# Cross-attention on one core: the query keys made for two batches at a time, in row halves, instead of one batch at a time with combined weights

## The chip, the core and the metric

The kernel runs on one core of a Trainium2 chip. The metric is the device time of one execution in microseconds. The chip's five engines run side by side and meet at semaphores: TensorE (PE, matmuls; PEld are its weight loads), VectorE (DVE), ScalarE (ACT), GpSimd (POOL) and SyncE (SP), whose queue issues nearly all DMAs. Each engine takes its instructions in order, so an instruction that waits holds back all behind it.

## What is computed

A perceiver block on 32 batches of 64 latents and 1601 context tokens of width 128: cross attention with 16 heads of 64, a self attention, and a quantized feed-forward. Only the first bears on the change:

```python
def _L0_xattn_ref(x, latents, mask, ...):       # x: context (32, 1601, 128), latents (32, 64, 128)
    xn, ln = layernorm(x, ...), layernorm(latents, ...)
    q = ln @ Wq                                 # 16 heads of 64
    kv = concatenate((xn, ln), axis=1) @ Wkv
    k, v = split(kv, 2, axis=-1)
    q, k, v = (heads(q) * scale, heads(k), heads(v))
    sim = einsum('bhid,bhjd->bhij', q, k)
    sim = where(mask_full[:, None, None, :], sim, max_neg)
    out = einsum('bhij,bhjd->bhid', softmax(sim), v)
    return layernorm(out @ Wout, ...)
```

## The kernel before

**Which keys.** The mask keeps only keys near the end of each context. A flag computed at the start picks one of two plans; with these inputs all keys before the last 448 are masked, and the plan WINDOW runs: 448 context keys and the 64 latents, in 8 steps per batch. A body is a pair of batches, 16 steps (0 to 7 the even batch's scores, 8 to 15 the odd one's). Bodies 0 and 1 are written out, 2 to 14 are a loop, 15 is written out again.

**Queries against keys.** The score of a latent against a key is taken as (A ln) . key, where A = Wq Wk^T per head is a 128x128 matrix. The setup forms A for 16 heads and two kinds of keys (context and latents), as fp16 high part a_h and low part a_l (lines 953, 752, 1295). Per batch, 4 query jobs multiply it with the 64 latents: for 8 heads each, three matmuls of 64 columns per head (lines 999, 1000, 1001: high x high, high x low, low x high). ScalarE copies the bank as a high part (qkc_h, line 780, for context keys; qkl_h, line 782, for latent keys), VectorE subtracts it from the bank for the low part (lines 1409, 1411).

**Jobs.** Preparation of the next batch is a row of jobs in two PSUM banks, jbank, used in turn: T (4 transposes of the normalised context, line 992, emptied to xtT_h and xtT_l, lines 770 and 1402), the 4 query jobs, 8 MAX jobs (lines 1014 and 1015: a row's scores for its maximum, reduced by VectorE, line 1415) and MT (the maxima transposed, line 1018, copied to mT, line 1422). A table sets at which step each stands: T at 0, queries at 0, 1, 1, 2, MAX from 2 to 5, MT at 6, the same in both halves of a body. TensorE makes a job when the last but one has been emptied (s_jobs_taken), so one bank is emptied while the other is filled.

**The steps.** In each step TensorE issues scores (lines 1045, 1047, 1049; step 0 adds the mask row, line 1053), then jobs of that step, then the values of two steps before (line 1072, fp32), then jobs of half steps, then the "tail" of the pairs before: ST1 (line 1101), ST2 (line 1109), self attention scores SC (line 1126), PT (transposes, line 1137), PV (line 1144) and small ones. ScalarE takes in each step the jobs of the half step before, the exp of the scores (line 794), the jobs of the step, the copies of the values (lines 800, 807) and its tail: the self attention's exp EXP (line 830) and PT_OUT (line 834). EXP waits for a maximum on VectorE (line 1486) and a subtraction on GpSimd (line 690).

**DMAs.** SP loads per batch the latents lnT, the context raw, ltT and lt, the maxima's row into mrow and into row 127 of qkc_h (lines 471 to 474), and moves the denominators through HBM (lines 482 to 496).

## Time and profile before

| | us |
|---|---|
| median of 3 runs | 965.45 |
| lowest, highest | 964.99, 966.32 |
| the profiled execution | 965.88 |
| its span, first to last instruction | 964.1 |

TensorE is busy in 855.6 us of the span (89%), VectorE in 597.5, ScalarE in 447.2, GpSimd in 189.4. In a timeline row the first number is the start in microseconds from the span's start, the second the time from the first start to the last end of the merged instructions. A matmul's record includes the way through the array, so neighbouring records overlap; what a matmul occupies is the distance between starts. An fp32 matmul stands as two records. "128\*64" behind MATMUL is rows x columns of the array.

### The profile page before, as it was taken

What the parts mean: (1) busy time and instruction counts of PE and PEld (TensorE: products, weight loads), DVE (VectorE), ACT (ScalarE), POOL (GpSimd) and SP (SyncE); (2) the same over time, 40 slices, a digit from 0 to 9 for tenths busy, and PEclk for the clock granted to TensorE, in tenths of its full rate; (3) what the DMA queues carried; (4) which work ended last, traced back from release to release, by engine and by line L of the source; (5) the groups of instructions that cost most, each with busy time, mean ns of one, the idle gap of its engine ahead of it and who ended that gap; (6) DMA issues with size and microseconds to landing.
All of it is one profiled execution on the core that took longest, in us unless ns stands there. A gap on an engine that the chain in (4) does not pass through costs nothing.

```text
span 964.1 us, 23144 instructions
## 1 busy us (share of the span) xinstructions
PE 855.6 (89%) x7999; PEld 487.7 (51%) x7999; DVE 597.5 (62%) x1564; ACT 447.2 (46%) x731; POOL 189.4 (20%) x351
## 2 busy tenths in 40 slices
PE   3658999999999999999999999999999999996452
PEld 3434554554655565646465555555554655555212
DVE  6857655566566656565757575767576666533377
ACT  2423545354545454555555454545454645451133
POOL 3110012121212212222222121212121212121200
PEclk9958999999999999999999999999999999998555
DMA  4221111111011101011111111111111011000001
GB/s 144 67 102 47 41 33 29 33 28 29 20 30 28 31 19 40 17 28 30 28 25 29 30 28 31 28 31 28 31 28 30 18 30 28 15 13 16 2 1 44
DMA packets 94246, 31.53 MB, mean 33 GB/s; under 512 B 77728, under 2 KB 92928, under 8 KB 94080
## 3 DMA queue, kind: packets, MB, share of 16 engines
q1 hardware_dynamic: 93584, 31.00, 13.1%
q8 instruction: 20, 0.33, 0.1%
q10 hardware_dynamic: 624, 0.05, 0.1%
q14 instruction: 18, 0.15, 0.1%
HBM read 26.25 MB, written 4.32 MB: 32 GB/s over the span
## 4 chain that ended last, share of the span: by engine, by line
PE 72%; DVE 16%; ACT 4%; issue 3%; DMA 2%; DVEq 2%; POOL 1%; SPq 0%; POOLq 0%
PE bank L1072 19%; PE bank L1045 7%; PE bank L1101 6%; PE bank L1049 5%; PE bank L1047 5%; PE bank L999 3%; PE bank L1109 3%; PE bank L1144 3%; PE bank L1001 3%; PE bank L1015 3%; PE bank L1000 3%; DVE mx L1415 3%; DVE qkl_l L1411 2%; ACT qkl_h L782 2%; PE bank L992 2%
## 5 line engine op out<-in xcount | busy, mean ns | idle before, releaser
L794 ACT ACTIVATE p<-bank,maskbias 128x512 f32<-128x512 f32 x224 | 154.0, 688 | 262.5 <-PE bank L1049 257.9
L1072 PE MATMUL bank<-p,xv 128*128 128x512 f32 (+1 forms) x512 | 238.1, 617 | 0.0
L1415 DVE TENSOR_REDUCE mx<-bank 128x1 f32<-128x512 f32 x256 | 165.5, 684 | 53.9 <-PE bank L1015 53.7
L1411 DVE TENSOR_TENSOR qkl_l<-bank,qkl_h 128x512 f16<-128x512 f32 x64 | 44.3, 692 | 111.8 <-ACT qkl_h L782 103.1
L999 PE MATMUL bank<-lnT,a_h 128*128 128x64 f16 x1024 | 102.3, 195 | 0.5 <-DVE xtT_l L1402 0.2
L1000 PE MATMUL bank<-lnT,a_h 128*128 128x64 f16 x1024 | 102.0, 194 | 0.0
L1001 PE MATMUL bank<-lnT,a_l 128*128 128x64 f16 x1024 | 102.0, 194 | 0.0
L999 PEld LDWEIGHTS bank<-lnT,a_h 128*128 128x128 f16 x1024 | 92.1, 99 | 18.0 <-issue 13.0
L1000 PEld LDWEIGHTS bank<-lnT,a_h 128*128 128x128 f16 x1024 | 91.9, 99 | 4.0
L1001 PEld LDWEIGHTS bank<-lnT,a_l 128*128 128x128 f16 x1024 | 91.9, 99 | 0.0
L1045 PE MATMUL bank<-qkc_h,xtT_h 128*128 128x512 f16 (+1 forms) x256 | 87.3, 392 | 0.0
L1047 PE MATMUL bank<-qkc_l,xtT_h 128*128 128x512 f16 (+1 forms) x256 | 85.5, 382 | 0.0
L1049 PE MATMUL bank<-qkc_h,xtT_l 128*128 128x512 f16 (+1 forms) x256 | 85.4, 381 | 0.0
L1072 PEld LDWEIGHTS bank<-p,xv 128*128 128x128 f32 (+1 forms) x512 | 75.6, 190 | 15.7 <-issue 8.8
L1101 PEld LDWEIGHTS bank<-arena,wvF 128*64 128x64 f32 x1024 | 56.3, 139 | 50.3 <-issue 50.3
L1015 PE MATMUL bank<-xtT_h,qkc_h 128*128 128x448 f16 x256 | 81.5, 358 | 0.0
L1101 PE MATMUL bank<-arena,wvF 128*64 128x128 f32 x1024 | 71.0, 283 | 4.0 <-DVE arena L1482 4.0
L1014 PE MATMUL bank<-ltT,qkl_h 128*128 128x64 f16 x256 | 50.1, 196 | 16.4 <-ACT p L794 7.0
L1402 DVE TENSOR_TENSOR xtT_l<-bank,xtT_h 128x512 f16<-128x512 f32 x32 | 22.1, 692 | 67.0 <-ACT xtT_h L770 60.2
L642 POOL TENSOR_TENSOR ve<-mv,epsrow 128x4 f32<-128x4 f32 x32 | 6.5, 203 | 269.2 <-DVE mv L1385 269.2
L1014 PEld LDWEIGHTS bank<-ltT,qkl_h 128*128 128x128 f16 x256 | 25.0, 98 | 61.0 <-DVE qkl_l L1411 30.8
L1409 DVE SCALAR_TENSOR_TENSOR qkc_l<-bank,ident,qkc_h 128x512 f16<-128x512 f32 x64 | 47.8, 747 | 5.8 <-ACT qkc_h L780 2.6
(236 smaller groups left out, 1432.4 us busy)
## 6 DMA issues: line engine op xcount, KB each, us to landing
arena<-den_dram SPq DMA_DIRECT2D x64, 128.0 KB, 3.2
raw<-in_ctx SPq DMA_DIRECT2D x32, 192.0 KB, 2.3
raw<-in_ctx SPq DMA_DIRECT2D x64, 32.0 KB, 2.2
lt<-lt_dram SPq DMA_DIRECT2D x64, 31.8 KB, 2.0
arena<-in_L_xattn_Wkv SPq DMA_DIRECT2D x1, 1024.0 KB, 9.5
lnT_dram<-x_all SPq DMA_DIRECT2D x1, 1024.0 KB, 4.0
ltT_dram<-xf_all SPq DMA_DIRECT2D x1, 1024.0 KB, 4.0
ltT<-ltT_dram SPq DMA_DIRECT2D x32, 32.0 KB, 1.8
```

The costliest lines, as they stand in the source:

```text
L794: a.activation(p32[0:r, slot, :], sbank[t % SRING][0:r, :], ACT.Exp, bias=bias).then_inc(s_probs_ready, 1)
L999: mm(bk[:, col], a_h[:, cl, hh, :], lnT[:, 0, :], start=True, stop=False)
L1000: mm(bk[:, col], a_h[:, cl, hh, :], lnT[:, 1, :], start=False, stop=False)
L1001: op = mm(bk[:, col], a_l[:, cl, hh, :], lnT[:, 0, :], start=False, stop=True)
L1014: mm(bk[:, rest:rest + M], qkl_h[:, col], ltT[:, par, 0, :], start=True, stop=True)
L1015: op = mm(bk[:, 0:rest], qkc_h[:, par, col], xtT_h[:, par, 512 * part:plan.KEYS], start=True, stop=True)
L1045: op = mm(dst, keys_h, q_h[:, col], start=True, stop=False)
L1047: op = mm(dst, keys_h, q_l[:, col], start=False, stop=False)
L1049: op = mm(dst, keys_l, q_h[:, col], start=False, stop=tile > 0)
L1072: op = mm(bk[:, :], rows_of[at, :], p32[at, slot, :], start=tile < 2, stop=tile in (0, plan.TILES - 1))
L1101: op = mm(abank[q // 2][E * odd:E * odd + E, (c % 4) * P:(c % 4) * P + P], wvF[:, cl, col], z[:, :, col], start=cl == 0, stop=cl == 1)
L1415: v.tensor_reduce(mx[:, hq_tile, part:part + 1], bk[:, 0:width], AX.X, ALU.max).then_inc(s_jobs_taken, 1)
```

## The change

The combined weights A are gone. The queries are made in two stages, for both batches of the next pair at once (128 columns).

- **QP** (2 jobs, one bank each): q = Wq ln, 4 chunks of two heads per job, three matmuls of 128 columns per chunk (wq_h, wq_l against lnT). Emptied to q_h and q_l in fp16.
- **QC** (2 jobs, two banks each): per head, the 64 rows of the key weights wk_h, wk_l against the 64 rows of q_h, q_l of that head. The even head of a chunk lies in partitions 0 to 63, the odd one in 64 to 127; their matmuls alternate, the even heads' into one bank, the odd heads' into the other. 24 matmuls of 128 columns and 64 rows per job. This is the query against context keys.
- **QL** (2 jobs, two banks each): the same with the weights for latent keys, into qkl_h and qkl_l, which now have a slot per batch.

QC's results go to qkn_h and qkn_l, since the slots of qkc_h and qkc_l are still read; move_queries has SP copy them by two DMAs of 256 KB per batch when the slot's last scores are done. Only the first pair's go straight to qkc_h and qkc_l. The columns are now ordered with all even heads first. A job of n banks waits until all jobs but the last 2 - n have been emptied. The new table puts QP at steps 0 and 1 of a body, QC at 1.5 and 6.5, QL at 8.5 and 9.5, T of the even batch at 7.5 (before 8), MAX from 2.5 and 10.5. Ahead of the first body, START has T, both QP, both QC, both QL, then MAX and MT. The last body has none of the query jobs. In the setup the transposes of Wq and the 32 matmuls for A with their copies go; wq_h, wq_l and wk_h, wk_l are formed instead.

```diff
+        self.START = self.numbered(self.of_batch(0, at["START"]) + self.of_queries(at["START"]))
+        self.BODY = self.numbered(self.of_batch(1, at["ODD"]) + self.of_queries(at["NEXT"]) + self.of_batch(0, at["EVEN"]))
+        self.LAST = self.numbered(self.of_batch(1, at["ODD"]))
...
+    def of_queries(self, at):
+
+        return [(kind, None, half, at[kind][half], banks) for kind, banks in (("QP", 1), ("QC", 2), ("QL", 2)) for half in range(2)]
...
-    T=[0], Q=[0, 1, 1, 2], XV={2: (0, 4)}, MAX=[2, 2.5, 3, 3, 4, 4, 5, 5], MT=6,
...
+    NEXT=dict(QP=[0, 1], QC=[1.5, 6.5], QL=[8.5, 9.5]),
...
-            def load_queries(n):
-                sp.dma_start(lnT[:, :, :], lnT_dram[:, :, bass.ds(n * M, M)].rearrange("s d q -> d s q")).then_inc(s_lnT_loaded, 16)
+            def load_queries(plan, pair):
+                sp.wait_ge(s_jobs_made, plan.queries_through(pair - 1, "QP", 1))
+                sp.dma_start(lnT[:, :, :], lnT_dram[:, :, bass.ds(pair * 2 * M, 2 * M)].rearrange("s d q -> d s q")).then_inc(s_lnT_loaded, 16)
+
+            def move_queries(plan, pair, k):
+
+                sp.wait_ge(s_jobs_taken, plan.queries_through(pair, "QC", 1))
+                sp.wait_ge(s_scores_ready, (pair * 2 + k - 1) * plan.STEPS)
+                sp.dma_start(qkc_h[:, k, :], qkn_h[:, k, :]).then_inc(s_qk_moved[k], 16)
...
+                        if since and k == 0:
+                            move_queries(plan, i, 1)
+                        if k == 1 and not last:
+                            move_queries(plan, i + 1, 0)
+                        if k == 0 and not last:
+                            load_queries(plan, i + 1)
...
+                if kind == "early":
+                    act.wait_ge(s_in_wq, 16)
+                    a.activation(wq_h[:, :], wq_sb, ACT.Copy, scale=Q_IN).then_inc(s_wq_hi, 1)
+                if kind == "wk":
                     act.wait_ge(s_setup_made, setup_made(kind, k))
-                    dst = {"wq": wqT, "wk": wkF[k // 2], "wv": wvF[:, k // 2, :].rearrange("p (c d) -> p c d", d=D)}[kind]
...
+                    if job.kind == "QP":
+                        a.activation(q_h[:, 4 * job.index:4 * job.index + 4, :].rearrange("p c t -> p (c t)"), both[0][:, :], ACT.Copy, scale=Q_OUT).then_inc(s_qk_hi, 1)
+                    if job.kind == "QC":
+
+                        if happened(n - 1):
+                            for k in range(2):
+                                act.wait_ge(s_qk_moved[k], n * 32 - 32)
+                        for odd in range(2):
+                            dst = heads_of(qkc_h if i is None else qkn_h, job.index, odd)
+                            a.activation(dst, by_batch(both[odd]), ACT.Identity, bias=ident[:, 127:128]).then_inc(s_qk_hi, 1)
+                    if job.kind == "QL":
+                        for odd in range(2):
+                            a.activation(heads_of(qkl_h, job.index, odd), by_batch(both[odd]), ACT.Copy).then_inc(s_qk_hi, 1)
 
             def probs(plan, i, k, t):
...
-                    hf, cl = divmod(j - plan.JOB_Q, 2)
-                    for h in range(8):
-                        col, hh = slice(h * M, h * M + M), 8 * hf + h
-                        mm(bk[:, col], a_h[:, cl, hh, :], lnT[:, 0, :], start=True, stop=False)
-                        mm(bk[:, col], a_h[:, cl, hh, :], lnT[:, 1, :], start=False, stop=False)
-                        op = mm(bk[:, col], a_l[:, cl, hh, :], lnT[:, 0, :], start=False, stop=True)
...
+                if happened(g + job.banks - 2):
+                    pe.wait_ge(s_jobs_taken, g + job.banks - 2)
...
+                    for c in range(4 * job.index, 4 * job.index + 4):
+                        to, heads = bk[:, (c % 4) * P:(c % 4) * P + P], slice(c * P, c * P + P)
+                        mm(to, wq_h[:, heads], lnT[:, 0, :], start=True, stop=False)
+                        mm(to, wq_h[:, heads], lnT[:, 1, :], start=False, stop=False)
+                        op = mm(to, wq_l[:, heads], lnT[:, 0, :], start=False, stop=True)
+                if job.kind in ("QC", "QL"):
+                    cl = ("QC", "QL").index(job.kind)
+                    pe.wait_ge(s_jobs_taken, plan.through(i, last, "QP", None, job.index))
+                    for c in range(4 * job.index, 4 * job.index + 4):
+                        to = slice((c % 4) * M, (c % 4) * M + M)
+                        for w, q, first, final in ((wk_h, q_h, True, False), (wk_h, q_l, False, False), (wk_l, q_h, False, True)):
+                            for odd in range(2):
+                                rws = slice(E * odd, E * odd + E)
+                                op = mm(by_batch(both[odd])[:, :, to], w[rws, cl, c, :], q[rws, c, :].rearrange("p (k t) -> p k t", k=2), start=first, stop=final)
...
+                        if happened(b - 1):
+                            pe.wait_ge(s_qk_moved[par], (b - par) * 16)
+                    if part == 0 and hq_tile in (0, 2):
+                        pe.wait_ge(s_jobs_taken, plan.queries_through(n if par == 0 else n - 1, "QL", hq_tile // 2))
...
-            for k in range(8):
-                dve.wait_ge(s_setup_made, setup_made("A", k))
-                dve.wait_ge(s_a_hi, k + 1)
-                v.tensor_tensor(heads_of(a_l, k), by_head(setup_bank("A", k)), heads_of(a_h, k), ALU.subtract).then_inc(s_setup_dve, 1)
+            dve.wait_ge(s_wq_hi, 1)
+            v.scalar_tensor_tensor(wq_l[:, :], wq_sb, Q_IN, wq_h[:, :], ALU.mult, ALU.subtract).then_inc(s_wq_lo, 1)
...
+                    if job.kind == "QC":
+                        for odd in range(2):
+                            dve.wait_ge(s_qk_hi, n * QJOBS + QC_HI[job.index] + odd)
+                            hi, lo = (qkc_h, qkc_l) if i is None else (qkn_h, qkn_l)
+                            v.scalar_tensor_tensor(heads_of(lo, job.index, odd), by_batch(both[odd]), ident[:, 127:128], heads_of(hi, job.index, odd), ALU.add, ALU.subtract).then_inc(s_jobs_taken, 1)
```

TensorE in the loop's body, from the even batch's values at step 0 on. Before (p is p32, the exps; xv the context values):

```order
L1072 MATMUL bank<-p,xv 128x512
L1126 MATMUL bank<-arena,qT 64x512 x4
L1045 MATMUL bank<-qkc_h,xtT_h 64x512 x2
...
L999 MATMUL bank<-lnT,a_h 128x64
L1000 MATMUL bank<-lnT,a_h 128x64
L1001 MATMUL bank<-lnT,a_l 128x64
...
L1072 MATMUL bank<-p,xv 128x512
...
L1045 MATMUL bank<-qkc_h,xtT_h 128x512
```

After (arena is q_h or q_l in the rows of L1064):

```order
L1134 MATMUL bank<-p,xv 128x512
L1188 MATMUL bank<-arena,qT 64x512 x4
L1107 MATMUL bank<-qkc_h,xtT_h 64x512 x2
...
L1055 MATMUL bank<-lnT,wq_l 128x128
...
L1134 MATMUL bank<-p,xv 128x512
...
L1064 MATMUL bank<-arena,wk_h 128x2x64 x4
L1064 MATMUL bank<-arena,wk_l 128x2x64 x2
...
L1107 MATMUL bank<-qkc_h,xtT_h 128x512
L1109 MATMUL bank<-qkc_l,xtT_h 128x512
```

Where two query jobs stood ahead of step 1's values and one ahead of step 2's, QP1 (12 matmuls) now stands ahead of step 1's values and QC0 (24, in two banks) right behind them.

ScalarE in the loop's body, from the self attention's exp (L830, then L890) on. Before:

```order
L830 ACTIVATE arena<-arena 128x1024
...
L794 ACTIVATE p<-bank,zrow 128x512
...
L770 ACTIVATE xtT_h<-bank 128x512
...
L780 ACTIVATE qkc_h<-bank,ident 128x512
L800 ACTIVATE arena<-bank 128x512
...
L834 ACTIVATE arena<-bank 128x512
...
L794 ACTIVATE p<-bank,maskbias 128x512
...
L782 ACTIVATE qkl_h<-bank 128x512
```

After (L894 is PT_OUT, L874 moves the first latents' sums):

```order
L890 ACTIVATE arena<-arena 128x1024
...
L829 ACTIVATE xtT_h<-bank 128x512
...
L854 ACTIVATE p<-bank,zrow 128x512
L860 ACTIVATE arena<-bank 128x512
...
L874 ACTIVATE arena<-arena 128x1024
...
L894 ACTIVATE arena<-bank 128x512
...
L842 ACTIVATE qkl_h<-bank 128x2x256 x2
...
L854 ACTIVATE p<-bank,maskbias 128x512
```

T's copy moved ahead of the first scores' exp, still behind the self attention's exp; the two copies of QL0 stand behind PT_OUT and ahead of the next exp.

ScalarE ahead of the first body. Before:

```order
L770 ACTIVATE xtT_h<-bank 128x512
L780 ACTIVATE qkc_h<-bank,ident 128x512
L782 ACTIVATE qkl_h<-bank 128x512
L780 ACTIVATE qkc_h<-bank,ident 128x512
L782 ACTIVATE qkl_h<-bank 128x512
```

After:

```order
L829 ACTIVATE xtT_h<-bank 128x512
L831 ACTIVATE arena<-bank 128x512 x2
L839 ACTIVATE qkc_h<-bank,ident 128x2x256 x4
L842 ACTIVATE qkl_h<-bank 128x2x256 x4
L854 ACTIVATE p<-bank,zrow 128x512
```

Four copies for one batch's queries became ten for two batches', all ahead of the first exp.

## Rows read from the trace of the kernel before

**Rows 1.** Stretches: us, busy us (count) by engine, PEclk granted clock, DMA share, GB/s.
```profile
53.00:72.00 19.00, 12.72 (x125) 7.04 (x125) 11.27 (x27) 3.17 (x5) 2.92 (x8) 0.59 0.12 33
500.00:600.00 100.00, 97.92 (x948) 55.24 (x945) 64.33 (x164) 49.76 (x84) 22.19 (x40) 1.00 0.12 28
```
**Rows 2.** The mask row's instructions by its line.
```profile
L1053 PE MATMUL bank<-mrow,onesrow x64: 398/398/631, 71.5 to 847.7; 1*64 1x512 f16 x64
```
**Rows 3.** Timeline, TensorE: mask rows of two bodies, two query jobs, values.
```profile
519.29 0.40 PE L1053 MATMUL bank<-mrow,onesrow 1*64 1x512 f16 x2
...
523.64 0.20 PE L999 MATMUL bank<-lnT,a_h 128*128 128x64 f16 x1
...
525.05 1.10 PE L1072 MATMUL bank<-p,xv 128*128 128x512 f32 x2
525.99 0.38 PE L1045 MATMUL bank<-qkc_h,xtT_h 128*128 128x512 f16 x1
...
569.84 0.40 PE L1053 MATMUL bank<-mrow,onesrow 1*64 1x512 f16 x2
```
**Rows 4.** Timeline, TensorE: two neighbouring 512-column matmuls in fp16.
```profile
564.54 0.38 PE L1047 MATMUL bank<-qkc_l,xtT_h 128*128 128x512 f16 x1
564.76 0.38 PE L1049 MATMUL bank<-qkc_h,xtT_l 128*128 128x512 f16 x1
```
**Rows 5.** Timeline, TensorE: values in two row halves, and in one full tile.
```profile
531.03 0.70 PE L1072 MATMUL bank<-p,xv 64*128 64x512 f32 x2
...
531.56 0.59 PE L1072 MATMUL bank<-p,xv 64*128 64x512 f32 x2
...
532.09 1.09 PE L1101 MATMUL bank<-arena,wvF 128*64 128x128 f32 x16
...
561.08 1.02 PE L1072 MATMUL bank<-p,xv 128*128 128x512 f32 x2
561.94 0.27 PE L1148 MATMUL bank<-ident,cx 128*128 128x128 f32 x1
```
**Rows 6.** Timeline, TensorE: values of step 7, then column-halved scores.
```profile
542.67 1.02 PE L1072 MATMUL bank<-p,xv 128*128 128x512 f32 x2
543.62 0.41 PE L1045 MATMUL bank<-qkl_h,ltT 128*64 128x512 f16 x2
```
**Rows 7.** Timeline, ScalarE and VectorE: query jobs emptied.
```profile
524.55 0.60 ACT L782 ACTIVATE qkl_h<-bank 128x512 f16<-128x512 f32 x1
525.25 0.69 ACT L780 ACTIVATE qkc_h<-bank,ident 128x512 f16<-128x512 f32 x1
...
525.97 0.75 DVE L1409 SCALAR_TENSOR_TENSOR qkc_l<-bank,ident,qkc_h 128x512 f16<-128x512 f32 x1
```
**Rows 8.** Timeline, ScalarE: the self attention's exp and PT_OUT.
```profile
545.37 1.06 ACT L830 ACTIVATE arena<-arena 128x1024 f32<-128x1024 f32 x1 [1.81 <-POOL arena L690]
...
549.37 0.61 ACT L834 ACTIVATE arena<-bank 128x512 f32<-128x512 f32 x1
```
**Rows 9.** Timeline, TensorE: a wait at a MAX job; ST2, transposes, scores.
```profile
530.71 0.20 PE L1014 MATMUL bank<-ltT,qkl_h 128*128 128x64 f16 x1 [0.54 <-ACT p L794]
...
546.85 1.95 PE L1109 MATMUL bank<-wout_sb,arena 128*128 128x128 f32 x16
548.64 0.60 PE L1137 MATMUL bank<-ident,arena 128*128 128x128 f32 x4
549.17 0.41 PE L1045 MATMUL bank<-qkc_h,xtT_h 128*64 128x512 f16 x2
```
**Rows 10.** DMA issues: count, KB each, median us from issue to landing.
```profile
raw<-in_ctx SPq DMA_DIRECT2D x32, 192.0 KB, 2.3
```
**Rows 11.** Timeline, VectorE, ahead of the first body: T and the last query job.
```profile
55.16 0.69 DVE L1402 TENSOR_TENSOR xtT_l<-bank,xtT_h 128x512 f16<-128x512 f32 x1 [2.16 <-ACT xtT_h L770]
...
60.46 0.69 DVE L1411 TENSOR_TENSOR qkl_l<-bank,qkl_h 128x512 f16<-128x512 f32 x1 [0.19 <-ACT qkl_h L782]
```
**Rows 12.** VectorE's subtractions for A in the setup, by their line.
```profile
L1295 DVE TENSOR_TENSOR a_l<-bank,a_h x8: 679/682/692, 26.0 to 30.5; 128x512 f16<-128x512 f32 x8
```

More of the change, by code:

```diff
@@ L48 @@
 LATE = dict(scales=4, round=[5, 6], awT=8, fwT=[9, 10], fwdT=11, wdrow=12)
+Q_IN, Q_OUT, K_IN = 2.0 ** 4, 2.0 ** -8, 2.0
+QJOBS = 10
+QP_HI, QC_HI, QL_HI = (1, 2), (3, 5), (7, 9)
+Job = namedtuple("Job", "kind k index at first banks")
 class Plan:
@@ new lines, in prep @@
+            def prep(plan, i, last, t):
+                n = 0 if i is None else i + 1
+                for job in plan.jobs(i, last):
+                    if job.at != t or job.kind in ("MAX", "MT"):
+                        continue
+                    made = plan.base(i) + job.first + job.banks
+                    both = [jbank[(plan.IN_START * (i is not None) + job.first + c) % 2] for c in range(job.banks)]
+                    act.wait_ge(s_jobs_made, made)
+                    if job.kind == "T":
+                        m, width = job.index, min(4, plan.CH - 4 * job.index) * P
+                        a.activation(xtT_h[:, job.k, 512 * m:512 * m + width], both[0][:, 0:width], ACT.Copy).then_inc(s_xtT_hi, 1)
+                    if job.kind == "QP":
[10 more added lines that the diff above has]
+                            a.activation(heads_of(qkl_h, job.index, odd), by_batch(both[odd]), ACT.Copy).then_inc(s_qk_hi, 1)
@@ L1161, in body @@
                         b = i * 2 + k
[L1162 removed]
                         scores(plan, i, k, t)
[L1164 to L1165 removed]
+                        prep(plan, i, last, s)
                         background(plan, i, since, s, before_self_scores)
```

293 lines of the change are left out of this document (142 added, 151 removed).

## The prediction

> **What bounds the kernel now.** I read the stretches first, then TensorE in order of time, then the other engines around each place where the change puts something. In a stretch of the steady loop TensorE is busy 97.9 us of 100 at the granted clock 1.00 (2.4 GHz), VectorE 64 and ScalarE 50 [rows 1]. So whatever TensorE issues, or waits for, is time; VectorE and ScalarE only matter where TensorE catches up with them. The mask row of a batch's first scores (L1053) starts 64 times between 71.5 and 847.7 us, two per batch [rows 2]: 15.5 pairs in 776 us, 50.1 us per pair, with the first two pairs shorter; a body of the loop takes 50.55.
>
> A query job is 24 matmuls of 64 columns. Two of them run from 523.64 to 525.05 us [rows 3]: 1.41 us, 0.70 per job, 29.4 ns per matmul, each with its own weight load. A 512-column matmul takes 0.22 [rows 4]. The line through both gives 0.056 us for 128 columns.
>
> **TensorE's work, per pair.** Removed: 8 jobs x 0.70 = 5.6 us. Added: QP, 2 jobs of 12 matmuls of 128 columns, 24 x 0.056 = 1.34 us. QC and QL, 4 jobs of 24 matmuls, neighbours in different row halves and different banks. Do such halves run together? In the values of a 64-row tile both halves' first parts start together at 531.03, the second parts at 531.56 and the next instruction at 532.09 [rows 5]: 1.06 us for two matmuls of 512 fp32 columns, while one full one takes 0.86 (561.08 to 561.94). They overlap, at 0.53 per part where a full one needs 0.43, a factor of 1.24. For fp16 with 128 columns the trace has no row, so the bounds are 0.056 (full overlap) and 0.070 us (the factor 1.24) for a couple; I take 0.060, since a couple's output and moving rows are narrower than there. 4 x 12 x 0.060 = 2.9 us (2.7 to 3.4). Each entry to or exit from such a shape costs something: after values ending at 542.67 + 0.86 = 543.53 the column-halved scores start at 543.62 [rows 6], while at 561.94 the unhalved successor starts without a gap. 0.09 us, seven new ones (QC0, QL0 and QL1 stand between full shapes, QC1 before a halved one): 0.6 us. TensorE's net: 5.6 - 1.34 - 2.9 - 0.6 = 0.75 us less per pair (0.2 to 1.0).
>
> The Trainium skill (TensorE: Matmul & The Clock Gate, Back-to-back issue gap) gives about 81 ns per 128-column matmul in a stream where each has its weight load. By that QP would cost 1.9 and the couples 3.9 us, 6.4 with the changes of shape, and the net would be 0.8 us more instead of 0.75 less. Rows 3 speak against it: 29.4 ns with a load each.
>
> **New waits, per pair.** A job of two banks waits until every earlier job has been emptied by ScalarE and VectorE. Before, a job waited only for the last but one.
> - QC0 (step 1.5) stands behind QP1 (step 1) with one values matmul between, 0.94 us (525.05 to 525.99) [rows 3]. Emptying one job after TensorE has issued it at 525.05: ScalarE starts at 525.25, VectorE is done at 525.97 + 0.75 = 526.72 [rows 7], 1.67 us; QP1's copies are of the 0.60 and 0.72 kind, 1.55. The wait is 1.55 + 0.04 - 0.94 = **0.65 us**. Behind it on TensorE stand the scores of step 2 and all else.
> - QC1 (6.5) stands behind MT, whose row is copied while the values of step 6 run: nothing.
> - QL0 (8.5) needs T of the even batch (now 7.5) emptied. On ScalarE T's copy stands behind the exp of the self attention (L830), which starts at 545.37 for 1.06 [rows 8], timed by VectorE's maximum and GpSimd's subtraction. I count from the body's mask row at 519.29: the exp ends at 27.1, T's copy at 27.7, VectorE's at 28.4. TensorE: the values of step 7 ended at 543.53, 24.2 after the mask row [rows 6]; the four jobs up to there cost as much as the four before (2 x 0.67 + 2 x 0.72 against 2.8), QC0's wait and three changes of shape bring 0.9, so T starts at 25.1 at the latest; T 0.5, first scores 1.1, values 0.94 and a change: 27.7. Wait 0.7; if the exp keeps its place and TensorE is 0.3 earlier, 1.0. I take **0.85**.
> - QL1 (9.5) needs QL0 emptied, and on ScalarE QL0's two copies stand behind PT_OUT (L834), which waits for the transposes behind ST2. From the transposes (548.64), which end at 549.17 [rows 9]: PT_OUT 549.37 to 549.98 [rows 8], two copies 1.2, VectorE's second 0.69: 551.9. TensorE has scores 0.77 and values 0.94 meanwhile: 550.9. **1.0 us**.
> - The first maxima of a half wait as before: in the old body TensorE loses 0.54 us at 530.71 ahead of a maximum [rows 9], and the same queue of maxima stays; I count -0.1.
>
> Sum 2.4 us (1.2 to 3.2). Pair: 2.4 - 0.75 = +1.65 us; bodies 2 to 14, 13 x 1.65 = **+21.5 us**.
>
> **Copies to the slots.** Two DMAs of 256 KB per batch on SP's queue, ahead of the loads of queries, context and of the denominator rows. A 192 KB load lands 2.3 us after issue [rows 10]; with two issues of 0.6 and 2.6 each is in 4 us after the last scores of the slot's batch, and the first maximum needs it 2.5 steps on, 8 to 10 us. Context loads go out some 3 us later and have four steps to spare. I cost them at nothing; if that cover went, each half would wait the whole excess.
>
> **Start.** The queries of two batches are made before the first maximum, and nothing covers their emptying. Before: T is emptied at 55.16 + 0.69 = 55.85, the last query job at 60.46 + 0.69 = 61.15 [rows 11]: 5.3 us. After: QP0 hides behind T; QP1 1.3 (the stretch's clock is 0.59 [rows 1]) + 0.2 + 0.6 + 0.8 = 2.9; each two-bank job 0.75 to 1.4 + 0.2 + 0.69 + 0.05 + 0.67 + 0.75 + 0.05 = 3.2 to 3.8, four in a row since each waits for the last. 15.5 to 18.1 against 5.3: +10.2 to +12.8, **+11**. The first batch's maxima, shift row and all scores come after it. In the setup VectorE's 8 subtractions of 0.68 (0.60 apart) [rows 12] give way to 4 and one over 1024 columns, some 1.2: -1.2 us. Bodies 0 and 1 wait on latencies, not on TensorE: longer chains against fewer jobs, +0.5 (-2 to +2). The last body has no query jobs: -2.8 of TensorE, less what its other waits keep, **-2**.
>
> Sum: 21.5 + 11 - 1.2 + 0.5 - 2 = +29.8. The profiled execution took 965.88 us (span 964.1), 0.4 above the median of the three runs; 965.9 + 29.8 = 995.7, so **996**.
>
> **Rivals.**
> (a) The row halves do not overlap in fp16: 24 x 0.056 = 1.34 instead of 0.72 per job, +2.5 per pair, of which 0.6 disappears in the wait at QL0; 13 x 1.9 = +25, 1021 us. For it: no fp16 row. Against it: rows 5. 9%.
> (b) A 128-column matmul with new weights costs more than its columns. The nearest dearer row is ST2, 16 fp32 parts of 128 columns between 546.85 and 548.64 [rows 9], 0.112 each; half way from 0.056 to that, 0.084, adds 24 x 0.028 for QP and 48 x 0.024 for the couples, 1.8 per pair, of which 0.6 is again taken out of a wait: 996 + 13 x 1.2 = 1012. Against it: the 64-column jobs show no such charge. 6%. The Trainium skill's figure in the section named above lies near that middle.
> (c) Faster: the three waits vanish, because TensorE's cover at QC0, QL0 and QL1 is longer than the emptying. The place to look is QL0 and QL1, where one late wait can use up the next one's. 13 x -0.75 - 1.2 - 2 + 10 = -3: 962 us. It decides from waits under 0.1 us per pair, since the start and the ends cost 8 us, 0.64 per pair. Against it: 0.94 against 1.59 us at QC0, both from rows. 6%.
> (d) The slots' DMAs come late, for 128 rows of 2 KB land slower than a load or SP sits in another wait: 1 us at each half is +28, 1024 us. For it: SP is one queue. Against it: 8 us of cover. 4%.
> (e) The waits are half of what I count, since one replaces the next: 996 - 15 = 981. 15%; the forecast itself (985 to 1010) 57%. No change to be measured, between (c) and (e): 3%.
>
> **Numbers.** Faster by over 0.2% (about what a measurement of this kernel can tell from no change): 0.07, (c) and its neighbourhood; same 0.03; slower 0.90. Range 978 to 1015: forecast, (e), (b) and the bounds of the couple's price (13 x 0.5) and of the start; (a), (c) and (d) are left out.
>
> **What the profile after will show.** Steady body 52.2 us between two mask rows; TensorE's share in a steady stretch down to some 94% with the clock still 1.00; idle before QC0 0.65, QL0 0.85, QL1 1.0, for VectorE's last copy; 24 QC matmuls in 0.72 us; the mask row of batch 0 at 81 to 82 us instead of 71.5; no wait on the slots' DMAs. Wrong if the couples take 0.11, if the three waits are not there, or if the clock falls in the loop.

## The result, and the profile after

The changed kernel takes 1021.39 us, median of 4 runs (1019.63 to 1022.33), against 965.88 for the kernel before on the same chip: a ratio of 1.057, interval 1.055 to 1.059. It is slower, as forecast, but by 55.5 us where 30 were forecast, and outside the range. The profiled execution took 1020.62 us, its span is 1018.9.

Mask rows cut both spans into the same stretches. Their starts come from the timeline of TensorE (the line is L1115 now). Here are those of the changed kernel at the start of body 0, in its middle, at its end, and at the start of body 2 and of the last body:

```profile
82.40 0.63 PE L1115 MATMUL bank<-mrow,onesrow 1*64 1x512 f16 x2 [1.48 <-DMA qkc_h<-mT]
116.28 0.40 PE L1115 MATMUL bank<-mrow,onesrow 1*64 1x512 f16 x2
136.90 0.40 PE L1115 MATMUL bank<-mrow,onesrow 1*64 1x512 f16 x2 [0.29 <-DMA qkc_h<-mT]
186.78 0.40 PE L1115 MATMUL bank<-mrow,onesrow 1*64 1x512 f16 x2
882.14 0.40 PE L1115 MATMUL bank<-mrow,onesrow 1*64 1x512 f16 x2
904.42 0.40 PE L1115 MATMUL bank<-mrow,onesrow 1*64 1x512 f16 x2
```

And those of the kernel before that [rows 2, 3] lack, the end of body 0 and the start of body 2:

```profile
117.72 0.40 PE L1053 MATMUL bank<-mrow,onesrow 1*64 1x512 f16 x2
165.46 0.40 PE L1053 MATMUL bank<-mrow,onesrow 1*64 1x512 f16 x2
```

With the mask rows of before at 71.53, 822.57 and 847.74 the account is, in us:

| stretch | before | after | difference | forecast |
|---|---|---|---|---|
| up to the first mask row | 71.53 | 82.40 | +10.9 | +9.8 |
| body 0 | 46.19 | 54.50 | +8.3 | both +0.5 |
| body 1 | 47.74 | 49.88 | +2.1 | |
| bodies 2 to 14 | 13 x 50.55 | 13 x 53.49 | +38.3 | +21.5 |
| half of the last body | 25.17 | 22.28 | -2.9 | -2, with the row below |
| the rest | 116.4 | 114.5 | -1.9 | |

So the start is right within 1.1 us, the loop is short by 1.29 us per body, and body 0 by some 8. The timeline of TensorE in one steady body shows where (start, length, then in brackets the idle time ahead and what ended it):

```profile
507.74 0.40 PE L1115 MATMUL bank<-mrow,onesrow 1*64 1x512 f16 x2
508.07 0.66 PE L1046 MATMUL bank<-ident,raw 128*128 128x128 f32 x4
509.82 0.23 PE L1053 MATMUL bank<-lnT,wq_h 128*128 128x128 f16 x1 [1.09 <-DMA lnT<-lnT_dram]
...
513.98 1.08 PE L1134 MATMUL bank<-p,xv 128*128 128x512 f32 x2
515.63 0.29 PE L1064 MATMUL bank<-arena,wk_h 64*128 64x128 f16 x4 [0.57 <-DVE arena L1474]
...
516.40 0.39 PE L1107 MATMUL bank<-qkc_h,xtT_h 128*128 128x512 f16 x1
...
520.04 0.20 PE L1080 MATMUL bank<-ltT,qkl_h 128*128 128x64 f16 x1 [0.32 <-DVE mx L1487]
...
535.59 1.12 PE L1134 MATMUL bank<-p,xv 128*128 128x512 f32 x2
537.43 0.28 PE L1064 MATMUL bank<-arena,wk_h 64*128 64x128 f16 x4 [0.71 <-DVE xtT_l L1470]
...
541.39 1.12 PE L1134 MATMUL bank<-p,xv 128*128 128x512 f32 x2
543.19 0.29 PE L1064 MATMUL bank<-arena,wk_h 64*128 64x128 f16 x4 [0.68 <-DVE qkl_l L1483]
...
545.20 1.13 PE L1134 MATMUL bank<-p,lt 64*128 64x512 f32 x4
546.80 0.19 PE L1080 MATMUL bank<-ltT,qkl_h 128*128 128x64 f16 x1 [0.48 <-DVE qkl_l L1483]
```

A pair of fp32 values matmuls occupies 0.94 us, so QC0 waits 515.63 - 513.98 - 0.94 = 0.71 us, QL0 0.90 and QL1 0.86. These are the three waits of the forecast (0.65, 0.85, 1.0). A QC job is done in 516.40 - 515.63 = 0.77 us with its changes of shape. The wait that the forecast has not is the first: from T to QP0 are 1.75 us, where T's four transposes occupy 0.5, and what ended it is the load of the queries, lnT.

SP's queue in the same place, and the place of the same load in the kernel before:

```profile
506.22 0.54 SPq L514 DMA_DIRECT2D qkc_h<-arena  x1
...
507.69 0.39 SPq L508 DMA_DIRECT2D lnT<-lnT_dram  x1
```
```profile
530.90 0.44 SPq L461 DMA_DIRECT2D lnT<-lnT_dram  x1
```

The load is issued at 507.69, behind the two slot copies, and lands some 2 us later (median 2.0 us for 15 such loads); TensorE wants it at 508.6. From the first copy's issue to the load's are 1.47 us: that time on SP is what puts the load off; its own way is hardly longer than the median of 1.9 us that it takes where it goes ahead of the copies. The kernel before issued it at 530.90 for queries that it made after the mask row at 544.39, 13 us ahead. By groups of waits (us in total, times, longest) it stands 13 times with 1.0 us each (the idle time counts from the end of the record ahead, so it is some 0.15 us shorter than the wait by starts):

```profile
PE bank L1053 <- DMA lnT<-lnT_dram: 13.1, 13, 1.2
```

In body 0 the same load stands behind nine late weight loads as well. SP's first and last issues of that row, then TensorE:

```profile
81.43 0.37 SPq L592 DMA_DIRECT2D arena<-in_L_attn_Wq  x1
...
85.23 0.43 SPq L596 DMA_DIRECT2D arena<-in_L_ffn_w_down  x1
85.70 0.43 SPq L508 DMA_DIRECT2D lnT<-lnT_dram  x1
```
```profile
82.96 1.11 PE L1046 MATMUL bank<-ident,raw 128*128 128x128 f32 x4
88.22 0.26 PE L1053 MATMUL bank<-lnT,wq_h 128*128 128x128 f16 x1 [4.15 <-issue]
...
107.46 0.27 PE L1084 MATMUL bank<-ident,negm 128*8 128x128 f32 x1 [2.48 <-DVE negm L1490]
...
109.70 0.39 PE L1064 MATMUL bank<-arena,wk_h 64*128 64x128 f16 x4 [0.93 <-DVE mT L1494]
```

QP0 waits 4.15 us ("issue" here, but it starts 2.5 us after the load's issue). Later MT waits 2.48 us, which it did before too (2.58), and now QC1, with two banks, waits for MT's copy. The windows of the changed kernel (us, busy us by engine, granted clock, DMA share, GB/s) show the clock at the lower level (0.50, that is 1.2 GHz) from 82 to 90 us, where TensorE waits for the load, and TensorE busy 92.0 of 100 us in the steady loop, where it was 97.9 [rows 1], at the clock 1.00:

```profile
82.00:90.00 8.00, 3.45 (x20) 2.23 (x22) 0.69 (x1) 1.59 (x3) 0.00 (x0) 0.50 0.52 141
104.00:112.00 8.00, 4.59 (x34) 2.08 (x33) 7.52 (x30) 1.48 (x3) 1.25 (x3) 0.77 0.01 2
500.00:600.00 100.00, 92.01 (x765) 48.35 (x763) 60.73 (x155) 48.67 (x84) 21.45 (x38) 1.00 0.18 48
```

### The profile page after: what moved, and what is told of

The parts are those of the page before. It is cut to its first block, busy times and chain, and to the rows that moved or that the text cites. A ratio compares the mean times of both kernels' runs of the same rounds, so it can differ in the third digit from the quotient of the medians.

```text
span 1018.9 us, 20883 instructions
## 1 busy us (share of the span) xinstructions
PE 850.8 (84%) x6775; PEld 456.3 (45%) x6775; DVE 613.7 (60%) x1593; ACT 447.9 (44%) x754; POOL 190.4 (19%) x351
## 4 chain that ended last, share of the span: by engine, by line
PE 58%; DVE 17%; issue 10%; ACT 6%; DMA 4%; POOL 2%; SPq 2%; DVEq 1%; ACTq 0%; POOLq 0%
PE bank L1134 13%; PE bank L1163 6%; PE bank L1064 5%; PE bank L1107 5%; DVE mx L1487 4%; PE bank L1111 3%; PE bank L1109 3%; PE bank L1081 3%; PE bank L1206 3%; PE bank L1171 3%; DMA lnT<-lnT_dram 3%; DVE qkl_l L1483 2%; PE bank L1199 2%; ACT qkl_h L842 2%; PE bank L1188 2%
## 5 line engine op out<-in xcount | busy, mean ns | idle before, releaser
L1483 DVE TENSOR_TENSOR qkl_l<-bank,qkl_h 128x512 f16<-128x512 f32 x64 | 41.2, 686 | 99.6 <-ACT qkl_h L842 99.5
L1081 PE MATMUL bank<-xtT_h,qkc_h 128*128 128x448 f16 x256 | 88.1, 359 | 0.0
L1064 PE MATMUL bank<-arena,wk_h 64*128 64x128 f16 x1024 | 53.3, 224 | 37.5 <-DVE qkl_l L1483 11.7
L1064 PEld LDWEIGHTS bank<-arena,wk_h 64*128 64x128 f16 x1024 | 38.6, 97 | 86.4 <-DVE qkl_l L1483 23.5
L1080 PE MATMUL bank<-ltT,qkl_h 128*128 128x64 f16 x256 | 50.4, 197 | 21.5 <-DVE mx L1487 11.4
L1474 DVE SCALAR_TENSOR_TENSOR arena<-bank,arena 128x512 f16<-128x512 f32 x32 | 22.1, 691 | 59.3 <-ACT arena L831 59.3
L1479 DVE SCALAR_TENSOR_TENSOR arena<-bank,ident,arena 128x512 f16<-128x512 f32 x60 | 42.0, 739 | 20.3 <-ACT arena L839 20.3
L839 ACT ACTIVATE arena<-bank,ident 128x512 f16<-128x512 f32 x60 | 37.9, 683 | 35.6 <-PE bank L1064 35.6
L1064 PE MATMUL bank<-arena,wk_l 64*128 64x128 f16 x512 | 48.9, 223 | 0.0
L860 ACT ACTIVATE arena<-bank 128x512 f32<-128x512 f32 x64 | 38.5, 602 | 13.7 <-PE bank L1134 13.7
```

What stands on the lines that cost most here:

```text
L1064: op = mm(by_batch(both[odd])[:, :, to], w[rws, cl, c, :], q[rws, c, :].rearrange("p (k t) -> p k t", k=2), start=first, stop=final)
L1080: mm(bk[:, rest:rest + M], qkl_h[:, par, col], ltT[:, par, 0, :], start=True, stop=True)
L1081: op = mm(bk[:, 0:rest], qkc_h[:, par, col], xtT_h[:, par, 512 * part:plan.KEYS], start=True, stop=True)
L1479: v.scalar_tensor_tensor(heads_of(lo, job.index, odd), by_batch(both[odd]), ident[:, 127:128], heads_of(hi, job.index, odd), ALU.add, ALU. ...
L1483: v.tensor_tensor(heads_of(qkl_l, job.index, odd), by_batch(both[odd]), heads_of(qkl_h, job.index, odd), ALU.subtract).then_inc(s_jobs_tak ...
```

## Experiments

Times are medians; "before" beside the groups was 966.65, 966.57, 966.28 and 966.79 us. The mask-row periods stand beside them, since they show a loop body free of the start and the end.

| kernel | us | loop body, mean of 13 | body 0 |
|---|---|---|---|
| before | 965.9 | 50.55 | 46.2 |
| changed | 1021.4 | 53.49 | 54.5 |
| load first | 1000.1 | 52.33 | 50.6 |
| + small copies | 999.8 | 52.33 | 50.6 |
| + rows by threes | 1001.4 | 52.36 | 50.4 |
| + rows by twelves | 1025.5 | 53.71 | 51.8 |
| load first, steps | 982.9 | 50.97 | 50.0 |
| load first, T at 7 | 976.8 | 50.45 | 49.8 |
| the same steps, load late | 990.0 | 51.22 | 55.1 |
| T at 7, start turned | 974.7 | 50.45 | 51.4 |
| + maxima apart | 972.8 | 50.54 | 51.1 |
| start turned, maxima late | 966.6 | 49.91 | 51.9 |
| + rounding late | 961.1 | 49.91 | 45.0 |
| before, rounding late | 965.8 | 50.55 | 46.5 |

### The load's place in the queue

```diff
                 load_rows(plan, None, False, 0)
+                load_queries(plan, 1)
...
                         more = not (last and k == 1)
+                        if since and k == 0 and not last:
+                            load_queries(plan, i + 1)
                         if since and k == 0:
                             move_queries(plan, i, 1)
                         if k == 1 and not last:
                             move_queries(plan, i + 1, 0)
-                        if k == 0 and not last:
-                            load_queries(plan, i + 1)
```

> The changed kernel with one order on SP turned: the load of the next pair's queries (lnT) is issued ahead of the two slot copies in every body from the second on, and ahead of the nine late weight loads in the start. Nothing else moves. Theory A, the load's place in SP's queue is the term that the prediction missed: in the loop TensorE waits at the first QP job 1.26 us for this load, in the first body 4.15 us behind the weight loads. Gone: 13 x 1.26 = 16 in the loop, some 1 in body 1, 4 to 6 in body 0 (its tail runs at the lower clock): 1021.4 - 22 = 999 us (996 to 1003), loop body 52.2 us. Rival B, the next wait takes it over (the exp of the self attention and the two-bank jobs keep their own times): the body stays above 52.9 and the time above 1011.

Measured: 1000.08 us (999.22 to 1000.25), 21 us less; the loop body is 52.33 where 52.2 was expected. SP and TensorE at one body's start:

```profile
492.03 0.39 SPq L508 DMA_DIRECT2D lnT<-lnT_dram  x1
492.62 0.55 SPq L514 DMA_DIRECT2D qkc_h<-arena  x1
```
```profile
494.10 0.66 PE L1047 MATMUL bank<-ident,raw 128*128 128x128 f32 x4
494.59 0.22 PE L1054 MATMUL bank<-lnT,wq_h 128*128 128x128 f16 x1
...
495.26 1.09 PE L1135 MATMUL bank<-p,xv 128*128 128x512 f32 x2
```

QP0 follows T at 0.49 us. The load is issued 2.56 us before it is wanted (492.03 to 494.59), and the waits behind did not take the gain over: 1.16 of 1.26 us come back per body. Theory A holds, rival B falls. Counted from the issue of the maxima's row into qkc_h (490.78 here, 504.76 in the changed kernel), the load goes out after 1.25 us instead of 2.93.

### What the slot copies themselves cost

```diff
-                sp.dma_start(qkc_h[:, k, :], qkn_h[:, k, :])
-                sp.dma_start(qkc_l[:, k, :], qkn_l[:, k, :])
+                sp.dma_start(qkc_h[120:128, k, :], qkn_h[120:128, k, :])
+                sp.dma_start(qkc_l[120:128, k, :], qkn_l[120:128, k, :])
```

> As e1_load_first, and each slot copy carries 8 of its 128 rows (120 to 127) instead of all, so 16 KB instead of 256 KB; the other rows of the slots keep the first pair's queries, so the kernel leaves out nearly all of the copying. Issues, waits and their order stay. Theory A: the copies' bytes are hidden, as in the prediction: within 2 us of e1_load_first. Rival C: the copies' traffic costs time (a maximum that waits for the slot, or other transfers that land later beside them): 5 us or more below e1_load_first; at 1 us per half it would be 28.

Measured: 999.77 us (999.62 to 1000.7), body 52.33. A sixteenth of the bytes changes nothing. The copies' transfers are hidden; what cost time in the changed kernel was their place ahead of another transfer. Both copies are still issued here (0.68 and 0.64 us on SP), so this run says nothing on the time of the issues. Their rows in the changed kernel (count, KB each, median us to landing) lie near the 2.3 us of [rows 10]:

```profile
qkc_h<-arena SPq DMA_DIRECT2D x30, 256.0 KB, 2.4
qkc_l<-arena SPq DMA_DIRECT2D x30, 256.0 KB, 2.5
```

### Do the row halves overlap?

```diff
                     for c in range(4 * job.index, 4 * job.index + 4):
                         to = slice((c % 4) * M, (c % 4) * M + M)
-                        for w, q, first, final in ((wk_h, q_h, True, False), (wk_h, q_l, False, False), (wk_l, q_h, False, True)):
-                            for odd in range(2):
+                        for odd in range(2):
+                            for w, q, first, final in ((wk_h, q_h, True, False), (wk_h, q_l, False, False), (wk_l, q_h, False, True)):
```

> As e1_load_first, but in QC and QL jobs the 12 matmuls of the even heads (upper row half) come first and then the 12 of the odd heads (lower row half), so that only one neighbour pair per job is in different halves. Same work, same banks. If the halves overlap in the changed kernel: a job takes 24 x 0.056 = 1.34 us instead of 0.75, +0.6 per job, 4 jobs per pair, of which at QL0 0.6 can disappear in QL1's wait: +1.8 to +2.4 per pair, 14 pairs and four jobs of the start: 25 to 36 us above e1_load_first. Rival, they never overlapped and a couple is cheap for another reason: within 3 us of e1_load_first.

Measured: 1001.42 us (1000.82 to 1003.4), body 52.36 against 52.33: the loop is the same, and QC0 takes 0.79 us to the next instruction (500.61 to 501.40). The edit did not do what its expectation says: the loop over the halves went inside the loop over the four column blocks, so that they alternate by three matmuls. The next kernel puts it outside both.

```diff
-                    for c in range(4 * job.index, 4 * job.index + 4):
+                    for odd in range(2):
+                        for c in range(4 * job.index, 4 * job.index + 4):
...
-                            for odd in range(2):
```

> As e1_load_first, but in each QC and QL job the 12 matmuls of the even heads (upper row half, first bank) come first and then the 12 of the odd heads (lower row half, second bank). e3_rows_apart had in truth grouped them by three and three, since its loop over the heads stood outside, and its records still run in pairs that start 10 ns apart; so it did not take the overlap away. If the overlap is real and reaches over three matmuls but not twelve: 24 x 0.056 = 1.34 us per job instead of 0.73, +0.6 on each of 4 jobs per pair, of which some can disappear in QL1's wait: +1.8 to +2.4 per pair, 25 to 38 us above e1_load_first (1000.1). Rival, a 64-row matmul of 128 columns takes 0.03 us whatever runs beside it: within 3 us of e1_load_first.

Measured: 1025.51 us (1024.91 to 1025.74), 25.4 above the kernel with the load first. The forecast's 0.06 us per couple does rest on an overlap. QC0 in that kernel:

```profile
515.22 0.28 PE L1065 MATMUL bank<-arena,wk_h 64*128 64x128 f16 x2 [0.57 <-DVE arena L1475]
...
515.68 0.32 PE L1065 MATMUL bank<-arena,wk_h 64*128 64x128 f16 x4
515.81 0.25 PE L1065 MATMUL bank<-arena,wk_l 64*128 64x128 f16 x2
...
516.31 0.22 PE L1065 MATMUL bank<-arena,wk_l 64*128 64x128 f16 x1
```

The twelve of the upper half, 0.056 apart, would end theirs at 515.22 + 12 x 0.056 = 515.89. At 515.68 four start together, so the lower half begins four matmuls early; the job's starts span 1.1 us where alternating they span 0.63. In the program two matmuls with wk_h are always followed by one with wk_l; the four with wk_h and two with wk_l in a row are two such groups, one of each half, interleaved. So matmuls of the lower half start ahead of some of the upper half that stand before them in the program, the first of them ahead of three. Groups of three overlap in full, groups of twelve only at their border. The body grows by 1.38 us: four jobs at about 0.46, less what disappears in QL0's wait, 0.71 to 0.25:

```profile
537.49 0.28 PE L1065 MATMUL bank<-arena,wk_h 64*128 64x128 f16 x2 [0.25 <-DVE xtT_l L1471]
```

### The waits of the two-bank jobs

```diff
-    NEXT=dict(QP=[0, 1], QC=[1.5, 6.5], QL=[8.5, 9.5]),
+    NEXT=dict(QP=[0, 0.5], QC=[1.5, 6.5], QL=[9, 10]),
```

> As e1_load_first, with three steps of the table moved: QP1 from 1 to 0.5, QL0 from 8.5 to 9, QL1 from 9.5 to 10. More of TensorE's own work lies between a job and the two-bank job that waits until it is emptied: 1.7 us instead of 0.94 ahead of QC0 (needs 1.6), 1.7 ahead of QL0. Theory A (waits of two-bank jobs are counted right, 0.65 + 0.85 + 1.0, and are a matter of cover): QC0's goes, QL0's goes, QL1's falls to 0.4 to 0.8, the first maximum behind it gains 0.3: 1.2 to 1.9 us per pair, 17 to 26 us below e1_load_first. Rival: they are set by ScalarE's other work (the exp, PT_OUT), whose times don't move: only QC0's goes, 8 us below e1_load_first, or nothing.

Measured: 982.89 us (982.15 to 984.08), 17.2 less. QC0, QL0 and QL1 wait for nothing, and the first maximum behind QL1 waits 0.82 us instead of 0.48. That is Theory A; but five of the loop's bodies, every second one of the later ones, are 1.5 us longer than their neighbours (51.9 and 50.4). The same 4 us in two bodies, 51.9 us apart:

```profile
571.00:575.00 4.00, 3.84 (x41) 2.63 (x41) 2.09 (x6) 0.94 (x3) 0.74 (x2) 0.80 0.11 24
...
623.00:627.00 4.00, 3.93 (x45) 2.70 (x45) 2.81 (x8) 1.16 (x2) 0.74 (x2) 1.00 0.11 24
```
```profile
571.16 0.19 PE L1081 MATMUL bank<-ltT,qkl_h 128*128 128x64 f16 x1 [0.82 <-DVE qkl_l L1484]
...
573.49 0.63 PE L1110 MATMUL bank<-qkc_l,xtT_h 128*128 128x512 f16 x1
573.92 0.63 PE L1112 MATMUL bank<-qkc_h,xtT_l 128*128 128x512 f16 x1
```

Two neighbouring 512-column matmuls stand 0.43 apart instead of 0.22 [rows 4]: the granted clock is at its lower level for some 3.3 us, 2 us behind the wait. In the other body the wait is 0.79 and the clock stays.

QP1, now half a step behind T, waits 0.21 us for T's copy, which it did not before.

The next kernel moves the waits once more, T of the even batch included:

```diff
-    NEXT=dict(QP=[0, 0.5], QC=[1.5, 6.5], QL=[9, 10]),
-    EVEN=dict(T=[7.5], MAX=[10.5, 11, 11, 11.5, 12, 12, 12.5, 13], MT=14)
+    NEXT=dict(QP=[0, 0.5], QC=[1.5, 6.5], QL=[8, 9]),
+    EVEN=dict(T=[7], MAX=[10.5, 11, 11, 11.5, 12, 12, 12.5, 13], MT=14)
```

> As e4_steps, with T of the even batch at step 7 instead of 7.5, QL0 at 8 instead of 9, QL1 at 9 instead of 10. ScalarE's copy of T then stands ahead of the exp of the self attention, QL0's ahead of PT_OUT, and the first maximum (10.5) has 1.5 steps behind QL1 instead of half a step. In e4_steps two things were left in the loop: 0.8 us ahead of the first maximum in every body, and in every second body a stretch of some 3 us at half the granted clock right behind it, 1.5 us. If that stretch comes of the waits just before it, both go: 14 x 0.8 + 7 x 1.5 = 21 us below e4_steps, 962; QL1 may keep 0.3 per pair: 961 to 968. Rival, the clock's fall has nothing to do with that wait: 0.8 per pair only, 971.

Measured: 976.75 us (973.74 to 977.87), far from the 961 to 968 expected. The maximum's wait is gone and so are the falls of the clock in the profiled execution, the fastest of the four (bodies of 50.2 to 50.5), but half a step earlier T runs into QC1:

```profile
606.70 0.65 PE L1047 MATMUL bank<-ident,raw 128*128 128x128 f32 x4 [0.54 <-DVE arena L1480]
```

Without its falls of the clock the kernel with the first table had 50.4 as well: one wait was traded for another, and what was gained is the clock. That it was this wait that made the clock fall is not shown; a later kernel has one as long and no fall.

> The table of e6_steps_t7 in the changed kernel, with its own order on SP (the load of the queries behind the slot copies and behind the weight loads). If the late load and the waits of the two-bank jobs are separate terms, the load's wait stays whole at the first QP job, 1.2 us per body and 4 in the first, and adds to what the steps leave: 20 to 22 us above e6_steps_t7. Rival, the cover that the steps give hides part of it: 12 or less above.

This is the changed kernel with that table alone, and SP as it was. Measured: 990.04 us (989.35 to 991.48), 13.3 above, where 20 to 22 was expected for separate terms and 12 or less for the rival. Between the two. (The profiled executions lie 15.8 apart, since that of the other kernel is its fastest.) Body 0 pays in full (55.1 against 49.8), but in the loop the load costs 0.77 us, not 1.2. QP0 still waits for it,

```profile
494.13 0.23 PE L1053 MATMUL bank<-lnT,wq_h 128*128 128x128 f16 x1 [0.93 <-DMA lnT<-lnT_dram]
```

but QP1's wait of 0.21 for T's copy in the other kernel is gone here: the delay covers it. T's 0.54 and the maxima's 0.29 and 0.31 stay.

### The start, and a version without the loss

```diff
-    START=dict(T=[0], QP=[0, 0], QC=[1, 1], QL=[2, 2], MAX=[3, 3, 3, 3, 4, 4, 4, 5], MT=6),
+    START=dict(T=[0.5], QP=[0, 0], QC=[1, 1], QL=[2, 2], MAX=[3, 3, 3, 3, 4, 4, 4, 5], MT=6),
```

> As e6_steps_t7, and in the start both QP jobs stand ahead of T. TensorE is idle there for 8.5 us, since T waits for the normalised context of batch 0, and the QP jobs need only the latents. They then run in that idle time, and QC0 waits for T alone: the chain of two-bank jobs begins 2.6 us earlier, 2.6 us below e6_steps_t7 (1.5 to 4). Rival, VectorE holds the two copies of QP back behind the context's normalising, which it does first: under 1 us.

Measured: 974.68 us (971.69 to 975.94), 2.1 less, a difference smaller than the 4 us over which the runs of either kernel spread. The mask rows say more. The first comes 2.7 us earlier (79.4 for 82.1), as expected, but 1.6 of it are lost again in body 0, where the even batch's T and the scores behind it now run at the lower clock; the last comes 1.15 earlier (855.55 for 856.70). So 1.1 us are the edit's, below the 1.5 to 4 forecast, and the rest of the 2.1 lies behind the last mask row, where nothing was changed.

Then two tables for the maxima, both with the start turned:

```diff
-    ODD=dict(T=[0], MAX=[2.5, 3, 3, 3.5, 4, 4, 4.5, 5], MT=6),
+    ODD=dict(T=[0], MAX=[2.5, 3, 3.5, 3.5, 4, 4.5, 4.5, 5], MT=6),
...
+    NEXT=dict(QP=[0, 0.5], QC=[1.5, 6.5], QL=[9, 10]),
+    EVEN=dict(T=[7.5], MAX=[11, 11.5, 11.5, 12, 12.5, 12.5, 13, 13], MT=14)
```

> From e7_start, whose loop body of 50.47 us still holds five waits of TensorE: T for QC1's emptying 0.54, a third maximum of each half 0.31 and 0.33, QP1 0.21, the first maximum 0.18. Here T is back at 7.5, QL0 and QL1 are at 9 and 10 as in e4_steps, the first maximum of the even batch goes from 10.5 to 11, so that a whole step lies behind QL1, and in both halves no maximum is issued straight behind the one before the last. Theory (each wait is cover that is missing between a job and the one that needs its bank): T's 0.54 goes, of the first maximum's 0.8 in e4_steps 0.1 to 0.2 stays, the third maxima's 0.6 falls to 0.1 to 0.4: body 49.6 to 49.9, 8 to 11 us below e7_start (974.7): 964 to 967, the time of the kernel before. Rival: the maxima are now so close to the end of the half that MT and the mask row wait, or the clock falls as in e4_steps: 972 or more.

> From e7_start only the maxima's steps are changed (2.5, 3, 3.5, 3.5, 4, 4.5, 4.5, 5 and the same 8 steps later), T stays at 7 and QL at 8 and 9. Takes away the third maxima's 0.31 and 0.33 per body, puts 0 to 0.2 elsewhere: 6 to 9 us below e7_start, 966 to 969. Rival: VectorE is what the maxima wait for, and the wait turns up at a later one: 973 or more.

Measured: 966.55 us (963.83 to 968.37, 12 runs) for the first, as expected (964 to 967) and no difference from before (0.9999, 0.999 to 1.0008); 972.77 (972.5 to 973.12) for the second, next to its rival's 973: the wait at the third maximum turned up as 0.82 at a later one. The first has that too:

```profile
571.42 0.20 PE L1081 MATMUL bank<-ltT,qkl_h 128*128 128x64 f16 x1 [0.82 <-DVE mx L1488]
```

but T, QC and QL wait for nothing, nor does anything wait for the slots, and its steady window is nearly that of [rows 1]:

```profile
500.00:600.00 100.00, 97.15 (x832) 52.74 (x828) 66.39 (x170) 52.11 (x88) 22.22 (x40) 1.00 0.18 49
```

Body 0 is still 51.9 us long. VectorE rounds the late weights there, between the maxima and the copies of MT and QC1.

```diff
-LATE = dict(scales=4, round=[5, 6], awT=8, fwT=[9, 10], fwdT=11, wdrow=12)
+LATE = dict(scales=7, round=[8, 9], awT=8, fwT=[11, 12], fwdT=13, wdrow=14)
```

> As e9_maxima_late, and VectorE's rounding of the late weights in body 0 stands at steps 8 and 9 instead of 5 and 6 (its scales at 7, what follows it two steps later). In e7_start the rounding runs from 99.1 to 105.6 us, between the last maxima and the copies of the first batch's MT and of QC1: MT waits 2.49, QC1 1.11, T 2.24 us, and TensorE's clock falls to 0.50 behind it. Theory: body 0 of the changed kernel is longer than before's (49.8 against 46.2 in e6_steps_t7) because two-bank jobs stand behind that block; out of the way it gives 4 to 7 us below e9_maxima_late: 958 to 962, faster than the kernel before. Rival: what comes at steps 8 and 9 (QL0, the context's moments) waits for it instead: within 2 us of e9_maxima_late.

> The kernel before, with the rounding of the late weights at steps 8 and 9 of body 0 (scales 7, the rest two steps later), the same edit as in e11_round_late. There too MT waits 2.58 us in body 0 behind that block, but no two-bank job stands behind it, and body 0 lasts 46.19 us. Theory: the block cost the changed kernel more (6.9 us of body 0, by the mask rows of e9_maxima_late and e11_round_late) because QC1 and T wait for whole banks behind it and the clock falls; before gains only MT's wait, 2 to 3 us: 963 to 965. Rival: the rounding costs both the same: 959 to 961, and e11_round_late is no faster than this kernel.

Measured: 961.09 us (959.39 to 962.79), where 958 to 962 was expected, a ratio of 0.995 (0.993 to 0.996): the fastest kernel of the study. The kernel before with the same edit takes 965.79 (963.22 to 967.66), a ratio of 0.999 (0.998 to 1.000), 1 us where 2 to 3 was expected. So to move the block is worth 5.5 us here and about 1 in the kernel before. There the first half of body 0 became 3 us shorter (22.06 for 25.13), as MT's wait fell from 2.58 to 0.41, and the second gave 3.4 back (24.46 for 21.06): its first maximum now waits 2.38 us for the last query job's copy instead of 0.21. In the other kernel the first half of body 0 fell from 29.2 to 22.4 us, and the second stayed at 22.7; it has a new wait of 1.50 at its first maximum too, but its granted clock rose from 0.92 to 1.00. Why the two differ in that was not tested. The middle of body 0, without and with the edit:

```profile
109.65 0.63 PE L1116 MATMUL bank<-mrow,onesrow 1*64 1x512 f16 x2
```
```profile
102.59 0.40 PE L1116 MATMUL bank<-mrow,onesrow 1*64 1x512 f16 x2
```

Body 0 began at 80.5 and at 80.2.

## Why the prediction was off

- **The step that failed** is the sentence on the copies to the slots: "Two DMAs of 256 KB per batch on SP's queue, ahead of the loads of queries, context and of the denominator rows ... I cost them at nothing". The copies themselves were rightly costed at nothing (small copies: 0.3 us less in 1000), and the cover of the maximum and of the context loads was checked. For the load of the queries, which the same sentence names, no time of need was worked out. Before, it had 13 us; now TensorE wants it 0.9 us after its issue. It cost 1.16 us in each loop body, and with body 0's weight loads ahead of it 3.9 there and 2.9 in body 1 (54.5 to 50.6, 49.9 to 47.0): 15 + 7 = 22, and the kernel with the load first is 21 us faster. The forecast was 25.7 us too low, and 21.3 of that are this load. Of the other 4 to 5, by the mask rows, 3.2 lie in bodies 0 and 1, 1.7 in the loop and 0.8 in the start, and the end gives 1.1 back.
- Rival (d) had the queue, "the slots' DMAs come late", but at the maximum, with 4%, and I set 8 us of cover there against it. It priced 1 us at each half; the wait was 1.2 us once per body, at QP0. The forecast of "no wait on the slots' DMAs" held; it was the wrong line to look for.
- Rival (a), row halves that don't overlap, gave 1021 us, the measured time. That is chance: its mechanism is refuted by the 0.77 us of a QC job. The time alone would have pointed to the wrong cause.
- **The rest of the loop.** With the load out of the way the body is 52.33 against 52.2 forecast, 1.78 above before's where 1.65 was forecast. The three waits were right: QC0 0.71 (0.65), QL0 0.90 (0.85), QL1 0.86 (1.0), together 2.47. Two smaller terms were off and nearly cancel, which is luck. The maxima were put at -0.1; they wait 0.48, 0.32 and 0.31 us where before had 0.54 and 0.23 at MT, so +0.3: the first one behind QL1 waits for its emptying, a queue that the forecast took as unchanged. TensorE's own work is then 1.78 - 2.47 - 0.34 = -1.0 us per pair, where -0.75 (0.2 to 1.0) was forecast. The starts of the jobs say the same: a QC or QL job takes 0.77 to 0.78 us with the change of shape behind it, 3.1 per pair, where 2.9 and 0.6 for the changes of shape were counted.
- **The couples** were right, and rivals (a) and (b) wrong: 24 matmuls in 0.77 us, 0.057 per couple and 0.09 for the shape change behind them. The Trainium skill's 81 ns per 128-column matmul with its weight load (TensorE: Matmul & The Clock Gate, Back-to-back issue gap) doesn't hold for the QP jobs: in the kernel with the load first the 12 of QP0 start at 494.59 and the next instruction at 495.26, 56 ns each, as read from [rows 3, 4]. That section's formula for a single matmul, N/2.4 + 2.5 ns, gives 56 ns too, and the trace agrees with it.
- **The start** was forecast at +9.8 with the setup and is +10.9; the first mask row was expected at 81 to 82 and is at 82.4. T is emptied at 54.4 (before: 55.85), the last query job at 72.0 (61.15), 17.6 us for 5.3, within the 15.5 to 18.1 forecast. The last body's half and the rest give -4.8 where -2 was expected. The half's -2.9 stands in every kernel of the new plan; the -1.9 behind it does not (-0.2 with the load first), and no run explains it.
- In rival (c) the start and the first two bodies enter with +10, where the forecast has 11 + 0.5; with its own terms it comes to 964 or 965 us, not 962. Nothing hangs on it.
- **Body 0** was the second miss, +8.3 against +0.5 for both first bodies. 3.9 are the load. The other 4.4 are waits that before hasn't: with the load first the first half of body 0 is 4.9 us longer than before's, and in it QC0 waits 1.49 us, QC1 1.11 and T 0.53, while the maximum's 1.30 and MT's 2.49 stood before as well; the granted clock is 0.80 for 0.85. QC1's and T's waits stand behind VectorE's rounding, QC0's ahead of it. Out of their way the rounding gave 6.9 us of body 0 in the last kernel (51.9 to 45.0); with the steps of the changed kernel it wasn't tried, so how much of the 4.4 it is stays open. I had looked at the two-bank jobs' waits in the steady loop alone.
- The changed kernel's clock stayed at 1.00 in the loop, as expected.

What stays open: why the clock falls behind a wait of 0.82 us in some bodies of one table and in none of another, whose waits sum up to 1.4 us per body instead of 1.8. And why the timed runs of the kernels with T at 7, and of the one without the loss, spread over some 4 us. In general the longer runs show a lower mean granted clock (start turned: 971.69, 974.03, 975.32 and 975.94 us at 0.934, 0.930, 0.929 and 0.923; maxima late: 963.83 at 0.934, 968.37 at 0.926), so falls of the clock in some executions are likely, but each kernel has one profile, and no run shows where they are.
